# Macaron block on one core: normalized rows written by column blocks, and three small reorderings

## The chip, the cores and the metric

The kernel runs on one core of one Trainium2 chip. The metric is the device time of one execution in microseconds, as the median of several executions. A core has five engines that work side by side and wait for each other through semaphores: TensorE (PE, with its weight loads shown as PEld), VectorE (DVE), ScalarE (ACT), GpSimd (POOL) and SyncE (SP), which issues most of the DMAs. Each engine takes its instructions in the order in which they are written.

## What is computed

x is 2 sequences of 2048 tokens with 256 features, all in float32. LN is a layernorm without weights.

```
x1 = x  + 0.5 * ffn(LN(x))
x2 = x1 + attention(LN(x1))
x3 = x2 + 0.5 * ffn(LN(x2))

ffn(h):   prev = h shifted by one token (zero at a sequence's start)
          xr, xk = mu_r*h + (1-mu_r)*prev,  mu_k*h + (1-mu_k)*prev
          sigmoid(xr @ W_r.T) * (relu(xk @ W_k.T)**2 @ W_v.T)
attention(h), 16 heads of 16:
          q, k = relu(h @ Wq.T)/4, relu(h @ Wk.T)/4 ; v = h @ Wv.T ; u = silu(h @ Wu.T)
          kv = k.T @ v over the whole sequence (per head) ; o = q @ kv
          (o / rms(o) * u) @ Wo.T
```

## The kernel before

**Tiling.** The 4096 tokens are 8 blocks of 512 (4 token tiles of 128). A block passes through FFN 1, attention's projections and the sum over tokens; when a sequence's four blocks are summed, attention's output can follow, then FFN 2. An FFN instance has a number n: 0 to 7 is FFN 1 of block n, 8 to 15 is FFN 2 of block n - 8.

**Precision.** A product of two float32 operands is made of three products in the faster fp32r format. Each operand is split into a high part (a copy to fp32r, on ACT) and a low part (the difference, on POOL or DVE). The helper product (L1328, L1329, L1330) issues hi*hi, hi*lo and lo*hi. Names with _hi and _lo are these parts.

**The order of work** is written out by hand on each engine. In the loop over block i (1 to 5 on POOL, 1 to 6 on DVE and ACT) the pieces that matter here are:

- PE: ffn_k(i+1), waiting for g_acc of block i-1; transpose_b (rows of x1 turned); ffn_r; k_and_u (attention's k and u); ffn_v; gram(i-1), the sum over tokens of x1 times k; q_of. After block 3's gram, kv(0) multiplies the sum by Wv.
- ACT: activate_k (relu, then Square to act_hi), x2_high, previous (the shifted rows), sigmoids, mix_high, sigmoid_u and kt_high, normalize(i+2), x1_high(i) (waits for gram(i-1)), at i = 2 the high part of W_o (L848), relu_q.
- POOL: act_low(i) (two squares at L467, then two subtractions at L476), scales_a(i+2), k_low(i+1), kt_low(i-1), scales_b(i) (var_epsB, rstdB), x1_low(i), at i = 2 the low part of W_o (L573).
- DVE: stats_a, turn(i+1), x2_low, mix_current, silu, gate and add of FFN 1, stats_b(i), r_low(i+1) (two subtractions to mix_r_lo), at i = 3 the centring of Wv, keep_g(i-1) (L1091 and L1094: gram's PSUM result into g_acc).

**Turned rows.** For n = 3 to 6 the normalized rows xn are not transposed on PE. SP stores them to a DRAM buffer `spread` (L390) in two halves, and loads them back into `squares` (L397), so that DVE can turn blocks of 32x32 into PSUM (turn, L989). ACT wrote xn (L646), and turn's output is what previous and mix_current read.

Of the kernel before, what the change touches and what calls it, by code (L numbers as in the profile page):

```python
# [5 lines left out]
F32 = mybir.dt.float32  # L6
# [39 lines left out]
def macaron(nc, x, w_t, mu_r, mu_k, out):  # L46
# [6 lines left out]
    with ExitStack() as ctx:  # L53
# [200 lines left out]
        def tile_row(tile, block, t):  # L254
            return row(tile, block, t * D, D)
# [27 lines left out]
        def parts(n):  # L283


            return 2 * (n - 1)
# [14 lines left out]
        quads = squares[:].rearrange("p g e -> p (g e)")  # L301
        spread = nc.dram_tensor("spread", [len(TURNED), 2, QUADS, P, P], F32).ap()

        def half(g):
            return slice(g * D, (g + 1) * D)

# [52 lines left out]
        @block.sync  # L359
        def _(sp):  # L360
            def load_x(b):
                sp.dma_start(row(xs, b).rearrange("p (t d) -> p t d", t=TILES),
                             x[b * BLOCK:(b + 1) * BLOCK, :].rearrange("(t p) d -> p t d", p=P)
                             ).then_inc(s_x_in[b], 16)

            def store_x(b):
                sp.wait_ge(s_x3, 2 * (b + 1))
                sp.dma_start(out[b * BLOCK:(b + 1) * BLOCK, :].rearrange("(t p) d -> p t d", p=P),
                             row(xs, b).rearrange("p (t d) -> p t d", t=TILES)).then_inc(s_out, 16)


            for t in (0, 2):
                sp.dma_start(tile_row(xs, 0, t), x[t * P:(t + 1) * P, :]).then_inc(s_x0[t], 16)
            sp.dma_start(raw_ffn[:, 0, :, :], weight_rows("ffn_k")).then_inc(s_w_in["ffn_k"], 16)
            load_x(1)
            sp.dma_start(raw_ffn[:, 1, :, :], weight_rows("ffn_r")).then_inc(s_w_in["ffn_r"], 16)
            sp.dma_start(raw_att[:, 0, :, :], weight_rows("k")).then_inc(s_w_in["k"], 16)
            sp.dma_start(raw_att[:, 1, :, :], weight_rows("u")).then_inc(s_w_in["u"], 16)
            sp.dma_start(raw_ffn_v[:], weight_rows("ffn_v")).then_inc(s_w_in["ffn_v"], 16)
            sp.dma_start(raw_att[:, 2, :, :], weight_rows("q")).then_inc(s_w_in["q"], 16)  # L380
            sp.dma_start(wv[:], weight_rows("v")).then_inc(s_w_in["v"], 16)
            load_x(2)
            sp.dma_start(wo[:], weight_rows("o")).then_inc(s_w_in["o"], 16)
            for b in range(3, NB):
                load_x(b)
            for k, n in enumerate(TURNED):
                for g in range(2):

                    sp.wait_ge(*normalized(n, 2 * g + 1))
                    sp.dma_start(spread[k, g].rearrange("j p (q f) -> p q j f", f=QUAD),  # L390
                                 xn[:, 2 * g:2 * g + 2, :].rearrange("p t (h j f) -> p (t h) j f", h=HALVES, j=QUADS)
                                 ).then_inc(s_spread[g], 16)
                if k > 0:
                    sp.wait_ge(s_tA, 2 * n)
                for g in range(2):
                    sp.wait_ge(s_spread[g], 16 * (k + 1))
                    sp.dma_start(quads[:, g * BANK:(g + 1) * BANK],  # L397
                                 spread[k, g].rearrange("j (c i) e -> (j c) (i e)", i=QUADS)).then_inc(s_quads[g], 16)
            for b in range(NB - 1):
                store_x(b)  # L400
            for t in range(TILES):
                sp.wait_ge((s_x3_even, s_x3_odd)[t % 2], t // 2 + 1)
                sp.dma_start(out[(NB - 1) * BLOCK + t * P:(NB - 1) * BLOCK + (t + 1) * P, :],
                             tile_row(xs, NB - 1, t)).then_inc(s_out, 16)
            sp.wait_ge(s_out, 16 * (NB - 1 + TILES))
# [3 lines left out]
        def _(pool):  # L409
# [53 lines left out]

            def act_squares(n):
                for h in range(HALVES):
                    pool.wait_ge(s_act_hi, parts(n) + h + 1)
                    nc.gpsimd.tensor_tensor(act_k[:, h, :], act_k[:, h, :], act_k[:, h, :],  # L467
                                            ALU.mult).then_inc(s_sq, 1)

            def act_low(n, squares=True):  # L470
                if squares:
                    act_squares(n)
                for h in range(HALVES):

                    pool.wait_ge(s_sq, parts(n) + h + 1)
                    nc.gpsimd.tensor_tensor(act_lo[:, h, :], act_k[:, h, :], act_hi[:, h, :].bitcast(F32),  # L476
                                            ALU.subtract).then_inc(s_act_lo, 1)

# [22 lines left out]
            def kt_low(a):  # L501

                for g in range(2):
                    pool.wait_ge(s_kt_hi, 2 * (a - 1) + g + 1)
                    tiles = slice(2 * g, 2 * g + 2)
                    nc.gpsimd.tensor_tensor(k_lo[:, tiles, :], k_tok[:, tiles, :], k_hi[:, tiles, :].bitcast(F32),  # L506
                                            ALU.subtract).then_inc(s_kt_lo, 1)
# [53 lines left out]
            for i in range(1, 6):  # L561
                act_low(i)
                scales_a(i + 2)
                k_low(i + 1)
                if i > 1:
                    kt_low(i - 1)
                scales_b(i)
                x1_low(i)
                if i == 1:
                    weight_sum("v")  # L570
                if i == 2:
                    pool.wait_ge(s_wo_hi, 1)
                    nc.gpsimd.tensor_tensor(wo_lo[:], wo[:], wo_hi[:].bitcast(F32), ALU.subtract).then_inc(s_wo_lo, 1)  # L573
            norm_second(0)
            act_low(6)
            k_low(7)
# [45 lines left out]
        def _(act):  # L622
# [15 lines left out]
            def normalize(n, tiles=range(TILES)):  # L638
                b = FFN[n][1]
                act.wait_ge(s_lnA, 3 * n)  # L640
                if n > 0:
                    act.wait_ge(s_tA, 2 * n)
                for t in tiles:
                    if t in xn_vector.get(n, ()):
                        continue
                    nc.scalar.activation(xn[:, t, :], tile_row(xs, b, t), ACT.Identity,  # L646
                                         bias=shiftA[:, t:t + 1], scale=rstdA[:, t:t + 1]).then_inc(s_xn, 1)

            def first_column(n):
# [48 lines left out]
            def activate_k(n, halves=range(HALVES)):  # L698
                for h in halves:
                    act.wait_ge(s_k, 2 * n + h + 1)  # L700
                    if n == 1 and h == 0:

                        act.wait_ge(s_v, 2)
                    elif n > 0 and h == 0:
                        act.wait_ge(s_act_lo, lows(n - 1))
                    nc.scalar.activation(act_k[:, h, :], psK[:, h, :], ACT.Relu).then_inc(s_relu, 1)
                    act.wait_ge(s_relu, 2 * n + h + 1)
                    if n == 0:
                        nc.scalar.activation(act_k[:, h, :], act_k[:, h, :], ACT.Square).then_inc(s_act_first, 1)
                        continue  # L710
                    if n > 1 and h == 0:
                        act.wait_ge(s_v, 2 * n)
                    nc.scalar.activation(act_hi[:, h, :], act_k[:, h, :], ACT.Square).then_inc(s_act_hi, 1)

            def activate_k2(n):
                for h in range(HALVES):
# [110 lines left out]
            for i in range(1, 7):  # L827
                front(i, i + 1, i - 1)
                sigmoid_u(i - 1, 0)
                sigmoid_r(i, 1)  # L830
                sigmoid_u(i - 1, 1)
                if i > 1:
                    kt_high(i - 1, 0)
                sigmoid_u(i - 1, 2)
                sigmoid_u(i - 1, 3)
                if i > 1:
                    kt_high(i - 1, 1)
                if i == 6:
                    keep_g_rows(0)
                mix_high(i + 1, 1)  # L840
                if i <= 5:
                    normalize(i + 2)
                if i >= 5:
                    square_heads(i - 5)
                x1_high(i)
                if i == 2:
                    act.wait_ge(s_w_in["o"], 16)
                    nc.scalar.activation(wo_hi[:], wo[:], ACT.Identity).then_inc(s_wo_hi, 1)  # L848
                relu_q(i - 1)

            front(7, None, 6)
# [68 lines left out]
        def _(dve):  # L920
# [305 lines left out]
            for i in range(1, 7):  # L1226
# [15 lines left out]
                if i == 6:  # L1242
                    add_attention(0)
                stats_b(i)
                r_low(i + 1)
                if i == 3:
                    center_weight("v", 4)
                keep_g(i - 1)
                if i == 4:
                    mask_kv(0)  # L1250
                if i == 6:
# [474 lines left out]
```

## Time and profile before

| | |
|---|---|
| median of 3 runs | 307.89 us (307.72 to 310.2) |
| the profiled execution | 307.94 us, its span 306.2 us |
| TensorE clock granted | full speed in all 40 slices |
| DMA | 28416 packets, 15.05 MB, 17122 packets under 512 B |
| HBM written | 6.29 MB |

The span is the stretch that the profile covers; the execution's own time is 1.7 us more. In the views a PE instruction's duration is modelled and overlaps with the next one, so the distance from one start to the next is what shows PE's pace. Idle time in square brackets stands ahead of the instruction, with what released it.

### The profile page before, as it was taken

Reading aid. Unit: us, or ns where it says so; the run is one execution under the profiler, and the core shown is the slowest. Engines: PE = TensorE matmul, PEld = TensorE weight load, DVE = VectorE, ACT = ScalarE, POOL = GpSimd, SP = SyncE. Lnnn points to the kernel's source line nnn. Section 1 sums busy time; section 2 is a strip of 40 time slices with the busy share of each in tenths; the row PEclk is TensorE's granted clock in tenths of the full one; section 3 lists DMA queues with packets and bytes.
Section 4 is the critical chain, followed back from the end, with each engine's and each line's share of the span. In section 5 each row is a group of like instructions: output and inputs, shape, how many; then the busy total and the mean of one; then the engine's idle time right before and its main releaser. Section 6 shows DMA issues by size and latency. Waiting matters only on the chain.

```text
span 306.2 us, 5777 instructions
## 1 busy us (share of the span) xinstructions
PE 298.5 (97%) x2003; PEld 271.7 (89%) x2003; DVE 247.4 (81%) x601; ACT 235.5 (77%) x461; POOL 214.5 (70%) x237
## 2 busy tenths in 40 slices
PE   6999999999999999999999999999999999999995
PEld 4888879978988898998988998999999999999894
DVE  4899896677876966985993798596989798999695
ACT  3988949969779779689178368489797979699981
POOL 4598969779689489479168116736797979759823
PEclk9999999999999999999999999999999999999999
DMA  7950070070330510000000000000001101001123
GB/s 234 382 208 2 2 137 2 2 137 0 58 83 0 80 59 0 2 1 2 0 2 1 2 0 0 2 2 2 0 16 56 37 34 54 17 2 68 42 99 137
DMA packets 28416, 15.05 MB, mean 49 GB/s; under 512 B 17122, under 2 KB 27364, under 8 KB 28388
## 3 DMA queue, kind: packets, MB, share of 16 engines
q1 hardware_dynamic: 28096, 14.42, 16.7%
q8 instruction: 16, 0.26, 0.3%
q10 hardware_dynamic: 292, 0.26, 0.2%
q14 instruction: 12, 0.10, 0.1%
HBM read 8.39 MB, written 6.29 MB: 48 GB/s over the span
## 4 chain that ended last, share of the span: by engine, by line
PE 63%; DVE 16%; POOL 8%; ACT 7%; issue 3%; DMA 1%; ACTq 0%; DVEq 0%; POOLq 0%
PE psK L1328 6%; PE psX L1328 6%; PE psK L1330 6%; PE psK L1329 6%; PE psX L1330 6%; PE psX L1329 6%; PE psRV L1328 5%; PE psRV L1330 5%; PE psRV L1329 5%; DVE mix L978 3%; PE psA L1533 2%; PE psX L1546 2%; PE psK L1533 2%; PE psA L1345 2%; DVE gate L1054 2%
## 5 line engine op out<-in xcount | busy, mean ns | idle before, releaser
L978 DVE SCALAR_TENSOR_TENSOR mix<-psA,mu,mix 128x512 f32<-128x512 f32 x60 | 41.5, 744 | 10.0 <-ACT mix L663 10.0
L454 POOL TENSOR_TENSOR mix_k_lo<-mix,mix_k_hi 128x512 fp32r<-128x512 f32 x26 | 33.6, 1313 | 5.1 <-ACT mix_k_hi L696 5.1
L663 ACT ACTIVATE mix<-psA,one_mu 128x511 f32<-128x511 f32 x60 | 36.9, 697 | 0.0
L1328 PE MATMUL psRV<-ffn_hi,mix_r_hi 128*128 128x256 f32 x120 | 34.3, 286 | 0.0
L1330 PE MATMUL psRV<-ffn_hi,mix_r_lo 128*128 128x256 f32 x120 | 33.6, 280 | 0.0
L1329 PE MATMUL psRV<-ffn_lo,mix_r_hi 128*128 128x256 f32 x120 | 33.5, 279 | 0.0
L646 ACT ACTIVATE xn<-xs,shiftA,rstdA 128x256 f32<-128x256 f32 x53 | 27.9, 623 | 2.6 <-POOL shiftA L438 2.6
L1328 PE MATMUL psRV<-ffn_hi,act_hi 128*128 128x256 f32 x96 | 27.6, 287 | 0.2 <-POOL act_lo L476 0.2
L1330 PE MATMUL psRV<-ffn_hi,act_lo 128*128 128x256 f32 x96 | 26.8, 279 | 0.0
L1329 PE MATMUL psRV<-ffn_lo,act_hi 128*128 128x256 f32 x96 | 26.8, 279 | 0.0
L947 DVE BATCH_NORM_STATS2 statsA<-xs 128x6 f32<-128x256 f32 x64 | 22.4, 412 | 2.7 <-DMA xs<-x_dram 2.6
L1328 PE MATMUL psK<-mix_k_hi,ffn_hi 128*128 128x512 f32 x60 | 24.2, 404 | 0.2
L442 POOL TENSOR_SCALAR var_epsB<-meanvarB 128x4 f32<-128x4 f32 x8 | 4.0, 498 | 28.5 <-DVE meanvarB L972 28.5
L497 POOL TENSOR_TENSOR x_lo<-xs,x_hi 128x512 fp32r<-128x512 f32 x14 | 17.8, 1295 | 8.3 <-ACT x_hi L746 8.3
L1330 PE MATMUL psK<-mix_k_hi,ffn_lo 128*128 128x512 f32 x60 | 23.5, 392 | 0.0
L1329 PE MATMUL psK<-mix_k_lo,ffn_hi 128*128 128x512 f32 x60 | 23.5, 391 | 0.0
L1328 PEld LDWEIGHTS psRV<-ffn_hi,mix_r_hi 128*128 128x128 f32 x120 | 22.5, 187 | 0.5 <-issue 0.2
L1329 PEld LDWEIGHTS psRV<-ffn_lo,mix_r_hi 128*128 128x128 f32 x120 | 22.6, 188 | 0.2
L1330 PEld LDWEIGHTS psRV<-ffn_hi,mix_r_lo 128*128 128x128 f32 x120 | 22.5, 188 | 0.0
L506 POOL TENSOR_TENSOR k_lo<-k_tok,k_hi 128x512 fp32r<-128x512 f32 x14 | 18.5, 1328 | 4.4 <-ACT k_hi L751 4.3
L696 ACT ACTIVATE mix_k_hi<-mix 128x512 fp32r<-128x512 f32 x30 | 18.9, 659 | 1.9 <-DVE mix L978 1.8
L1328 PEld LDWEIGHTS psRV<-ffn_hi,act_hi 128*128 128x128 f32 x96 | 18.0, 188 | 0.7 <-POOL act_lo L476 0.4
(211 smaller groups left out, 1086.5 us busy)
## 6 DMA issues: line engine op xcount, KB each, us to landing
xs<-x_dram SPq DMA_DIRECT2D x7, 512.0 KB, 7.8
out_dram<-xs SPq DMA_DIRECT2D x7, 512.0 KB, 2.8
spread<-xn SPq DMA_DIRECT2D x8, 256.0 KB, 4.5
squares<-spread SPq DMA_DIRECT2D x8, 256.0 KB, 2.7
out_dram<-xs SPq DMA_DIRECT2D x4, 128.0 KB, 1.7
xs<-x_dram ACTq DMA_DIRECT2D x2, 128.0 KB, 3.1
xs<-x_dram SPq DMA_DIRECT2D x2, 128.0 KB, 2.8
silu_u<-w_ffn_k_dram SPq DMA_DIRECT2D x1, 256.0 KB, 4.0
```

Of the source, the lines that this page charges most:

```text
L454: nc.gpsimd.tensor_tensor(mix_k_lo[:, h, :], mix[:, 0, h, :], mix_k_hi[:, h, :].bitcast(F32), ALU.subtract).then_inc(s_lo_k, 1)
L497: nc.gpsimd.tensor_tensor(x1_lo[:, g * BANK:(g + 1) * BANK], row(xs, a, g * BANK, BANK), x1_hi[:, g * BANK:(g + 1) * BANK].bitcast(F32), A ...
L506: nc.gpsimd.tensor_tensor(k_lo[:, tiles, :], k_tok[:, tiles, :], k_hi[:, tiles, :].bitcast(F32), ALU.subtract).then_inc(s_kt_lo, 1)
L646: nc.scalar.activation(xn[:, t, :], tile_row(xs, b, t), ACT.Identity, bias=shiftA[:, t:t + 1], scale=rstdA[:, t:t + 1]).then_inc(s_xn, 1)
L663: nc.scalar.activation(mix[:, rk, h, 1:BLOCK], psA[:, h, 0:BLOCK - 1], ACT.Copy, scale=one_mu[:, rk, h:h + 1]).then_inc(s_prev, 1)
L696: nc.scalar.activation(hi[:, h, :], mix[:, rk, h, :], ACT.Identity).then_inc(done, 1)
L947: nc.vector.bn_stats(statsA[:, t, :], tile_row(xs, b, t)).then_inc(s_bnA, 1)
L978: nc.vector.scalar_tensor_tensor(out=m, in0=psA[:, h, :], scalar=mu[:, rk, h:h + 1], in1=m, op0=ALU.mult, op1=ALU.add).then_inc(s_mix, 1)
L1328: nc.tensor.matmul(dst, a_hi, b_hi, start=start, stop=False)
L1329: nc.tensor.matmul(dst, a_hi, b_lo, start=False, stop=False)
L1330: return nc.tensor.matmul(dst, a_lo, b_hi, start=False, stop=stop)
L1533: last = nc.tensor.matmul(ps[:, t // 2, (t % 2) * D + h * P:(t % 2) * D + (h + 1) * P], q_half(j, h)[:, tok(t)], kv_bd[:, j // BB, h, :], ...
```

## The change

- xn of n = 3 to 6 is written by ACT in another order: instead of a token tile's 256 features in a row, feature h*128 + j*32 + f goes to block j, so that block j of two token tiles lies in 128 neighbouring elements. The store then moves one piece of 128 elements (512 bytes) per partition and j, where it moved four of 32 elements. What lands in `spread` is the same.
- keep_g(i-1) stands ahead of r_low(i+1) (and of the centring of Wv) on DVE.
- The high part of W_o stands ahead of x1_high(2) on ACT, the low part ahead of scales_b(2) on POOL.
- Of FFN 1's instance n = 1, the second half's square in act_k is done by ACT behind act_hi, not by POOL. POOL's later waits on its own squares count one less.

```diff
+        def spread_rows(t):
+            return xn[:].rearrange("p t d -> p (t d)").rearrange("p (g j t h f) -> p g t h j f", g=2, j=QUADS, t=2, h=HALVES
+                                                                 )[:, t // 2, t % 2, :, :, :]
...
-                    sp.dma_start(spread[k, g].rearrange("j p (q f) -> p q j f", f=QUAD),
-                                 xn[:, 2 * g:2 * g + 2, :].rearrange("p t (h j f) -> p (t h) j f", h=HALVES, j=QUADS)
+                    sp.dma_start(spread[k, g].rearrange("j p e -> p j e"),
+                                 xn[:, 2 * g:2 * g + 2, :].rearrange("p t d -> p (t d)").rearrange("p (j e) -> p j e", j=QUADS)
                                  ).then_inc(s_spread[g], 16)
...
             def act_squares(n):
                 for h in range(HALVES):
+                    if (n, h) == (1, 1):
+                        continue
                     pool.wait_ge(s_act_hi, parts(n) + h + 1)
...
-                    pool.wait_ge(s_sq, parts(n) + h + 1)
+                    if (n, h) == (1, 1):
+                        pool.wait_ge(s_act_first, HALVES + 1)
+                    else:
+                        pool.wait_ge(s_sq, parts(n) + h + 1 - (n > 1))
...
                 if i > 1:
                     kt_low(i - 1)
+                if i == 2:
+                    pool.wait_ge(s_wo_hi, 1)
+                    nc.gpsimd.tensor_tensor(wo_lo[:], wo[:], wo_hi[:].bitcast(F32), ALU.subtract).then_inc(s_wo_lo, 1)
                 scales_b(i)
                 x1_low(i)
                 if i == 1:
                     weight_sum("v")
-                if i == 2:
-                    pool.wait_ge(s_wo_hi, 1)
-                    nc.gpsimd.tensor_tensor(wo_lo[:], wo[:], wo_hi[:].bitcast(F32), ALU.subtract).then_inc(s_wo_lo, 1)
...
-                    nc.scalar.activation(xn[:, t, :], tile_row(xs, b, t), ACT.Identity,
+                    given, rows = tile_row(xs, b, t), xn[:, t, :]
+                    if n in TURNED:
+                        given, rows = given.rearrange("p (h j f) -> p h j f", h=HALVES, j=QUADS), spread_rows(t)
+                    nc.scalar.activation(rows, given, ACT.Identity,
                                          bias=shiftA[:, t:t + 1], scale=rstdA[:, t:t + 1]).then_inc(s_xn, 1)
...
                     nc.scalar.activation(act_hi[:, h, :], act_k[:, h, :], ACT.Square).then_inc(s_act_hi, 1)
+                    if (n, h) == (1, 1):
+                        act.wait_ge(s_act_hi, HALVES)
+                        nc.scalar.activation(act_k[:, h, :], act_k[:, h, :], ACT.Square).then_inc(s_act_first, 1)
...
-                x1_high(i)
                 if i == 2:
                     act.wait_ge(s_w_in["o"], 16)
                     nc.scalar.activation(wo_hi[:], wo[:], ACT.Identity).then_inc(s_wo_hi, 1)
+                x1_high(i)
                 relu_q(i - 1)
...
                 stats_b(i)
+                keep_g(i - 1)
                 r_low(i + 1)
                 if i == 3:
                     center_weight("v", 4)
-                keep_g(i - 1)
```

## Rows read from the trace of the kernel before

**Rows 1.** The page: busy time, share of the span and instructions

```profile
PE 298.5 (97%) x2003; PEld 271.7 (89%) x2003; DVE 247.4 (81%) x601; ACT 235.5 (77%) x461; POOL 214.5 (70%) x237
```

**Rows 2.** Timelines of POOL and PE, gram(1): start us, us, line, tiles, count

```profile
58.13 1.31 POOL L506 TENSOR_TENSOR k_lo<-k_tok,k_hi 128x512 fp32r<-128x512 f32 x1
...
59.59 0.28 PE L1330 MATMUL psK<-k_hi,x_lo 128*128 128x256 f32 x1
59.70 0.28 PE L1328 MATMUL psK<-k_hi,x_hi 128*128 128x256 f32 x1
```

**Rows 3.** Timeline of PE in ffn_v(1)

```profile
34.66 0.28 PE L1330 MATMUL psRV<-ffn_hi,act_lo 128*128 128x256 f32 x1
35.18 0.39 PE L1328 MATMUL psRV<-ffn_hi,act_hi 128*128 128x256 f32 x1 [0.24 <-POOL act_lo L476]
35.41 0.28 PE L1329 MATMUL psRV<-ffn_lo,act_hi 128*128 128x256 f32 x1
```

**Rows 4.** Timeline of PE from q_of(0) to ffn_k(2); PE and weight load at ffn_k(3)

```profile
43.51 0.39 PE L1329 MATMUL psX<-x_lo,att_hi 128*128 128x512 f32 x1
43.74 0.39 PE L1330 MATMUL psX<-x_hi,att_lo 128*128 128x512 f32 x1
44.17 0.50 PE L1328 MATMUL psK<-mix_k_hi,ffn_hi 128*128 128x512 f32 x1
...
64.35 0.39 PE L1330 MATMUL psX<-x_hi,att_lo 128*128 128x512 f32 x1
64.87 0.19 PEld L1328 LDWEIGHTS psK<-mix_k_hi,ffn_hi 128*128 128x128 f32 x1 [0.55 <-DVE g_acc L1094]
```

**Rows 5.** Timeline of PE in gram(2)

```profile
80.77 0.28 PE L1330 MATMUL psK<-k_hi,x_lo 128*128 128x256 f32 x1
81.20 0.39 PE L1328 MATMUL psK<-k_hi,x_hi 128*128 128x256 f32 x1 [0.15 <-POOL k_lo L506]
```

**Rows 6.** Timeline of PE from q_of(3) to kv(0)

```profile
106.23 0.39 PE L1330 MATMUL psX<-x_hi,att_lo 128*128 128x512 f32 x1
106.70 0.68 PE L1511 MATMUL psA<-wv,g_acc 128*128 128x128 f32 x4
```

**Rows 7.** Timeline of POOL, act_low(1)

```profile
30.56 2.04 POOL L467 TENSOR_TENSOR act_k<-act_k 128x512 f32<-128x512 f32 x2
```

**Rows 8.** Timeline of ACT in block 1; groups by line and shape

```profile
27.31 0.63 ACT L713 ACTIVATE act_hi<-act_k 128x512 fp32r<-128x512 f32 x1
...
L635 ACT ACTIVATE att_hi<-q_store 128x512 fp32r<-128x512 f32 x3 | 1.7, 613 | 0.0
```

**Rows 9.** Timeline of DVE in block 1

```profile
37.27 1.66 DVE L1061 TENSOR_TENSOR xs<-xs,gate 128x512 f32<-128x512 f32 x1
...
42.25 1.26 DVE L1019 TENSOR_TENSOR mix_r_lo<-mix,mix_r_hi 128x512 fp32r<-128x512 f32 x2
43.43 0.68 DVE L1091 COPY g_acc<-psK 128x512 f32<-128x512 f32 x1
```

**Rows 10.** Timelines of DVE and PE in block 6

```profile
151.41 1.26 DVE L1019 TENSOR_TENSOR mix_r_lo<-mix,mix_r_hi 128x512 fp32r<-128x512 f32 x2
...
151.83 0.38 PE L1533 MATMUL psA<-kv_bd,q_store 128*128 128x128 f32 x2
```

**Rows 11.** Timeline of POOL in block 2, then in block 7

```profile
63.13 0.54 POOL L442 TENSOR_SCALAR var_epsB<-meanvarB 128x4 f32<-128x4 f32 x1 [3.68 <-DVE meanvarB L972]
...
67.83 1.28 POOL L573 TENSOR_TENSOR wo_lo<-wo,wo_hi 128x512 fp32r<-128x512 f32 x1
...
177.34 0.20 POOL L442 TENSOR_SCALAR var_epsB<-meanvarB 128x4 f32<-128x4 f32 x1 [6.15 <-DVE meanvarB L972]
```

**Rows 12.** Timeline of ACT in block 2

```profile
62.08 1.06 ACT L746 ACTIVATE x_hi<-xs 128x1024 fp32r<-128x1024 f32 x1 [1.17 <-PE psK L1330]
```

**Rows 13.** DMA issues: KB each, median us from issue to landing

```profile
spread<-xn SPq DMA_DIRECT2D x8, 256.0 KB, 4.5
squares<-spread SPq DMA_DIRECT2D x8, 256.0 KB, 2.7
```

## Prediction

> **What bounds the kernel now.** I read the busy table first: TensorE 97% against 81, 77 and 70% for VectorE (DVE), ScalarE (ACT) and GpSimd (POOL) [rows 1]. Every product runs on TensorE (PE) and the change touches none, so only PE's gaps can be won. The modelled ends hide them: a 256-column product is listed with 0.28 us while the next starts 0.12 us later. So I went through PE's own timeline start to start. Undisturbed pitches are 0.12 us for 256 columns [rows 2] and, in the second gap's rows below, 0.23 us for 512. Starts of neighbours that I give without a group are read from the same engine's timeline and only place an instruction. From 30 to 120 us five gaps stand out:
>
> - 34.66 to 35.18: 0.52 us where 0.12 is usual, lost 0.40; the product behind it takes 0.23 instead of 0.12, 0.11 more. Releaser: act_lo on POOL [rows 3]. Together 0.51.
> - 43.74 to 44.17: 0.43 against 0.23, lost 0.20, plus the 0.11 of restart: 0.31. ffn_k(2) waits there for keep_g(0) [rows 4].
> - 64.35 to 64.87: 0.52 against 0.23, 0.29 + 0.11 = 0.40. ffn_k(3) waits for keep_g(1), the releaser of its weight load after 0.55 us idle [rows 4].
> - 80.77 to 81.20: 0.43 against 0.12, 0.31 + 0.11 = 0.42. gram(2) waits for the second k_lo on POOL [rows 5].
> - 106.23 to 106.70: 0.47 against 0.23, 0.24. kv(0) waits for keep_g(3) [rows 6]. I count no restart here, because kv's plain fp32 products have another pitch.
>
> Sum 0.51 + 0.31 + 0.40 + 0.42 + 0.24 = 1.88 us. Everything else that PE loses is in the opening (before 30 us) or after 220 us, where the change edits nothing. So 1.9 us, 0.6% of the time, is close to all that this change could win.
>
> **The change, part by part.**
>
> *One square of block 1 to ACT.* POOL now does two squares (2.04 us) and then two subtractions ahead of the first gap [rows 7]. Taking one square away (1.02 us) brings the second act_lo 1.0 us forward; PE wants it 0.51 earlier, so the gap closes whole: -0.51. On ACT the square costs one more Square of 128x512, 0.63 us [rows 8]; it follows act_hi at about 27.95 and ends near 28.6, three microseconds before POOL asks. Queued behind it are previous(2), the sigmoids and all of sigmoid_u(0). ACT has no idle time until its normalizations at 37.2, so they move by the 0.63. What consumes them: DVE's mix and silu, then gate_ffn(1). The gate starts at 36.55 having idled 0.57 for PE, so DVE absorbs most of the 0.63. gram(0) on PE needs k_tok, which ends at 35.1 now and 35.7 then, against a start at 37.8 less 0.5. Cost on the path: nothing; if that cover were gone, at most 0.63.
>
> *keep_g ahead of r_low.* In each block DVE runs two r_low subtractions (1.26 us) before keep_g (0.68 us) [rows 9]. The swap makes g_acc final 1.2 us earlier. The three waits that it feeds are short by 0.31, 0.40 and 0.24, so all three close: -0.95. What is put later is mix_r_lo, by 0.6 us, to about 44.1 in block 1, and its consumers (ffn_r(2) at 47.8, the copies of previous(3) at 49.4) are over three microseconds away. The added risk is that keep_g now waits for gram, with r_low, the statistics and the turn queued behind it on DVE. In blocks 1 to 5 gram is done before DVE gets there (block 1: gram ends about 41.1, DVE arrives at 42.25). In block 6 it is not: DVE arrives at 151.41 and PE leaves gram(5) at 151.83 [rows 10], so DVE idles about 0.55. The chain behind it ends in head_norms(1) and x2_low(6); k_and_u(6) wants x2_low only at 162.8, and it is done 0.4 before, after waiting 0.2 for ACT, so 0.6 of room against 0.55. I take 0, and up to +0.1 for the range.
>
> *W_o's split moved.* wo_lo (1.28 us) now stands in POOL's chain just ahead of act_squares(3), behind which k_low(4) and the late k_lo follow. In its new place, before scales_b(2), POOL has been idle for 3.68 us [rows 11]. wo_hi on ACT (a copy of 128x512, 0.61 us by the nearest row [rows 8]) goes in front of x1_high(2), where ACT idles 1.17 us for gram [rows 12], so x1_high starts when it did. wo_lo then runs from about 61.5 to 62.8, before var_epsB at 63.1. Both copies are hidden, with 0.3 us to spare on POOL. POOL becomes free 1.28 earlier, and the 0.42 gap closes: -0.42. If the 0.3 were missing, POOL would still gain over 0.9, so the gap closes anyway.
>
> *Rows by column blocks.* ACT writes the same 256 elements in runs of 32 instead of one run; the store's pieces go from 128 to 512 bytes, 2048 to 512 of them. For ACT's price the nearest row is a copy whose output is cut in runs (att_hi, two runs of 256): 0.61 us for 512 elements, where an uncut one takes 0.63 [rows 8]. I take no change; the bounds are 0 and, for runs 8 times shorter than that row shows, +0.1 us per write. Four writes then take 0.4 of the 1.2 us or more that ACT idles behind them, so still nothing on the path. For the store: it lands 4.5 us after issue, and the reload of the same bytes, in 2 KB pieces, 2.7 [rows 13]. I take about 3, between them and near the reload, so the turned rows arrive some 1.5 us earlier. DVE's waits for them go. None of it is PE time today, because x2_low behind the turn waits for ACT anyway. But PE reaches block 3 some 1.2 us earlier after the edits above, and without faster turned rows it would be short by about 0.3 there. So this edit is worth 0 alone and protects the others.
>
> The page "SBUF — State Buffer" of the Trainium skill (Reading the diagram) states that a VectorE instruction with two SBUF inputs and a GpSimd one that reads SBUF exclude each other for a whole instruction. The trace agrees: DVE's add at 37.27 takes 1.66 us instead of 0.69 while POOL runs k_low(2) [rows 9]. By that rule POOL's k_low(2), once it starts earlier, could block the add anew at another moment and the sum would be 306.7 (the second rival); by my reading of the row the overlap shrinks and the sum stays 306.0.
>
> **What is next late.** PE reaches gram(1) 0.82 us (0.51 + 0.31) earlier. Its third token tile starts at 59.7 now, 58.9 then, and the second k_lo runs from 58.13 for 1.31 us [rows 2], to 59.45. So k_lo must come 0.55 us earlier or a new gap opens. POOL's chain from block 1's second layernorm is solid work, so it must start that much earlier. Two things push that way. DVE's adds in block 1, which took 1.66 and about 1.0 us beside POOL, meet less of it, since k_low(2) starts and ends 1.0 earlier (my estimate is 0.5 us). And POOL's var_epsB takes 0.54 us when r_low runs on DVE beside it [rows 11], against 0.20 in block 7, where DVE runs an instruction that reads PSUM [rows 11]; keep_g reads PSUM too, so another 0.3 or so. Estimate 0.8, enough by a quarter of a microsecond.
>
> **Sum.** Against the profiled execution: 307.94 us (span 306.2, with 1.7 around it) - 0.51 - 0.95 - 0.42 = 306.06. The median of the runs shown is 307.89, 0.05 lower; so 306.0.
>
> **Rivals.**
> - *Faster than the sum.* An opening that moves, or a tail that closes: the late gaps (about 0.3 us near 223, three near 290 to 300 of together 0.8) belong to chains that shift with PE, so I see no cause. 305.3.
> - *The new wait at gram(1).* If POOL's chain in block 1 comes no earlier (DVE's adds blocked at other moments), 0.55 + 0.11 returns: 306.7. With the turned rows also no faster, 0.3 more: 307.0. For it: the margin is 0.25 and rests on contention. Against: var_epsB's shorter time alone gives half.
> - *Nothing.* The gaps are handed on, gate by gate, to the DVE-ACT chains that alternate from 275 us to the end in the chain view: 307.9. Against: PE starts stay at their pitch through almost all of 110 to 220 us, so PE itself sets when those chains begin.
> - *Slower.* ACT's writes in runs of 32 cost double: 0.5 us each, 2.1 us per block in blocks 1 to 4, against 1.2 us of idle time behind them, so x1_high, relu_q and through it the transposes of x1 come 0.9 late four times: +3.6, less 0.9 for the gaps that still close: 310.6. It decides from 0.3 us per write. The uncut and cut rows of ACT speak against it.
> - *The change doesn't do what it says:* pieces are 512 bytes but landing is latency, 4.5 stays; that is in the second rival.
>
> **Chances.** The forecast (306.0, give or take 0.4) 0.58; faster 0.07; the new wait 0.20; nothing 0.11; slower 0.04. A change within 1% (3.1 us) is about what a measurement of this kernel can't tell from none. Faster by over 1% would need 304.8, more than all the gaps: 0.03. Slower by over 1% needs 311.0, the slower rival at its upper end: 0.03. Same 0.94. The range leaves out the slower rival and part of "faster" and of "nothing": 305.3 to 307.8.
>
> **What the profile after would show.** Right: no PE gap before the second half of ffn_v(1), at ffn_k(2), ffn_k(3), the third tile of gram(2), or kv(0); wo_lo between kt_low(1) and var_epsB; var_epsB near 0.2 us in blocks 1 to 5; the store landing in 3 us with 512-byte packets; no DVE wait for squares; the xn writes still at 0.62. Wrong: a PE gap with k_lo as its releaser at gram(1) near 59, xn writes above 0.9 us, or a DVE idle of over 0.6 before keep_g(5) that reaches k_and_u(6).

## The result, and the profile after

The median of 16 runs is 306.73 us (305.67 to 308.03) against 308.98 us (307.48 to 310.39) for 16 runs of the kernel before on the same chip: ratio 0.9934, 95% interval 0.9912 to 0.9957. The profiled execution took 305.97 us with a span of 304.2, against 307.94 and 306.2. Forecast were 306.0 in a range of 305.3 to 307.8. The forecast started from 307.89, the median of three runs; over 16 runs the medians differ by 2.25 us and the lowest runs by 1.81, where 1.9 was forecast. The median of the kernel after falls between two clusters of runs (eight at 306.35 or less, eight at 307.11 or more; last section), and so does that of the kernel before.

The page of the kernel after, busy time, clock, packets and the chain that ended last:

```profile
PE 297.3 (98%) x2003; PEld 272.1 (89%) x2003; DVE 245.9 (81%) x601; ACT 236.0 (78%) x462; POOL 210.8 (69%) x236
...
PEclk9999999999999999999999999999999999999999
...
DMA packets 16128, 15.05 MB, mean 49 GB/s; under 512 B 738, under 2 KB 15076, under 8 KB 16100
...
PE 85%; DVE 8%; ACT 3%; issue 1%; DMA 1%; POOL 1%; DVEq 0%; ACTq 0%
...
spread<-xn SPq DMA_DIRECT2D x8, 256.0 KB, 3.4
squares<-spread SPq DMA_DIRECT2D x8, 256.0 KB, 2.7
```

TensorE's share hardly moves (97% to 98%, [rows 1]), but the gaps are gone. PE's own timeline of the kernel after, at the five places:

```profile
34.72 0.28 PE L1346 MATMUL psRV<-ffn_hi,act_lo 128*128 128x256 f32 x1
34.84 0.28 PE L1344 MATMUL psRV<-ffn_hi,act_hi 128*128 128x256 f32 x1
...
43.30 0.39 PE L1346 MATMUL psX<-x_hi,att_lo 128*128 128x512 f32 x1
43.52 0.39 PE L1344 MATMUL psK<-mix_k_hi,ffn_hi 128*128 128x512 f32 x1
...
63.58 0.39 PE L1346 MATMUL psX<-x_hi,att_lo 128*128 128x512 f32 x1
63.80 0.39 PE L1344 MATMUL psK<-mix_k_hi,ffn_hi 128*128 128x512 f32 x1
...
79.52 0.28 PE L1346 MATMUL psK<-k_hi,x_lo 128*128 128x256 f32 x1
79.64 0.28 PE L1344 MATMUL psK<-k_hi,x_hi 128*128 128x256 f32 x1
...
104.57 0.39 PE L1346 MATMUL psX<-x_hi,att_lo 128*128 128x512 f32 x1
104.80 0.83 PE L1527 MATMUL psA<-wv,g_acc 128*128 128x128 f32 x6
```

The starts are 0.12 us apart for 256 columns and 0.23 for 512, where 0.52, 0.43, 0.52, 0.43 and 0.47 stood [rows 3 to 6].

**The measure used below.** Executions of one program differ by about 2 us before FFN 1's block 1 (last section), so spans of single profiles can't be compared. I take the stretch from the start of the first product of ffn_k(1) to the start of the last product of all. In the timeline of the kernel after these are:

```profile
21.02 0.58 PE L1344 MATMUL psK<-mix_k_hi,ffn_hi 128*128 128x512 f32 x1
...
300.32 0.28 PE L1346 MATMUL psK<-ffn_hi,act_lo 128*128 128x256 f32 x1
```

279.30 us. In the kernel before the same two start at 20.98 and 302.29: 281.31. The stretch lost 2.01 us. "At +49.8" means 49.8 us after the first of the two. Both kernels issue the same products in the same order, and the difference of their starts grows in steps, all at the five places: 0.50 behind the ffn_v(1) gap, 0.80 behind ffn_k(2), 1.23 behind ffn_k(3) (1.28 soon after), 1.71 behind gram(2), 2.02 behind kv(0), and then constant within 0.06 to the end.

### The profile page after: what moved, and what is told of

Its sections match the earlier page's. It is cut to its first block, busy times and chain, and to the rows that moved or that the text cites. A ratio compares the mean times of both kernels' runs of the same rounds, so it can differ in the third digit from the quotient of the medians.

```text
span 304.2 us, 5777 instructions
## 1 busy us (share of the span) xinstructions
PE 297.3 (98%) x2003; PEld 272.1 (89%) x2003; DVE 245.9 (81%) x601; ACT 236.0 (78%) x462; POOL 210.8 (69%) x236
## 4 chain that ended last, share of the span: by engine, by line
PE 85%; DVE 8%; ACT 3%; issue 1%; DMA 1%; POOL 1%; DVEq 0%; ACTq 0%
PE psK L1344 8%; PE psK L1346 8%; PE psK L1345 8%; PE psX L1344 8%; PE psX L1346 8%; PE psX L1345 8%; PE psRV L1344 8%; PE psRV L1346 7%; PE psRV L1345 7%; PE psA L1361 3%; PE psA L1549 2%; PE psX L1562 2%; PE psX L1476 2%; PE psK L1549 2%; DVE mix L994 2%
## 5 line engine op out<-in xcount | busy, mean ns | idle before, releaser
L447 POOL TENSOR_SCALAR var_epsB<-meanvarB 128x4 f32<-128x4 f32 x8 | 1.9, 238 | 26.4 <-DVE meanvarB L988 26.4
L789 ACT ACTIVATE q_store<-psX 128x512 f32<-128x512 f32 x16 | 9.6, 598 | 12.1 <-PE psX L1346 12.1
```

## The experiments

| kernel | median, us | lowest run | ratio of times | first and last product | stretch |
|---|---|---|---|---|---|
| before | 308.98 | 307.48 | | 20.98, 302.29 | 281.31 |
| after | 306.73 | 305.67 | 0.9934 | 21.02, 300.32 | 279.30 |
| after_again | 305.9 | 305.74 | 0.9895 [0.986, 0.993] | 21.08, 300.32 | 279.24 |
| no_rows | 307.53 | 305.41 | 0.9951 [0.9922, 0.998] | 22.86, 302.61 | 279.75 |
| no_keep_g | 308.0 | 306.82 | 0.9983 [0.9956, 1.001] | 20.79, 301.14 | 280.35 |
| no_wo | 307.36 | 305.8 | 0.9953 [0.9926, 0.9979] | 22.39, 301.68 | 279.29 |
| no_square | 306.3 | 305.91 | 0.9933 [0.9911, 0.9955] | 21.05, 300.96 | 279.91 |
| only_rows | 307.87 | 307.62 | 1.0002 [0.9974, 1.0029] | | |
| only_keep_g | 308.06 | 306.36 | 0.9988 [0.9967, 1.0009] | 20.80, 300.73 | 279.93 |
| only_wo | 307.77 | 307.63 | 0.9987 [0.9964, 1.0009] | 20.77, 302.13 | 281.36 |
| only_square | 307.09 | 306.79 | 0.9981 [0.996, 1.0003] | 22.65, 303.07 | 280.42 |
| rows_keep_g | 306.67 | 306.01 | 0.992 [0.9891, 0.9949] | 22.90, 302.53 | 279.63 |
| twice | 309.15 | 307.06 | 0.9977 [0.9947, 1.0007] | 20.82, 301.64 | 280.82 |
| norm_first | 311.4 | 310.16 | 1.0066 [1.0042, 1.0089] | 20.80, 304.64 | 283.84 |

Where a kernel gains or loses under 1 us the stretch decides, and the lowest run supports it: it lies 26.0 to 26.5 us above the stretch in all but no_rows (25.66). The medians carry the 2 us of the opening too. Each ratio compares a kernel with runs of the kernel before taken beside it, not with the table's first row: medians 308.04 (lowest 307.64) for no_rows, no_keep_g, no_wo and no_square, 308.05 (307.55) for the only_ kernels, 309.65 (307.75) for the other four.

A wait costs PE twice: the distance to the product behind it, beyond the usual one, and a restart of about 0.11 us at the next (0.07 to 0.08 at kv(0) and k_and_u(2)). Such pairs are added up below.

**after_again**: the kernel after, unchanged. It repeats to 0.06 us. By the expectation below, the 0.46 us of no_rows would then be its edit's; what speaks against that stands at no_rows.

> The kernel after, unchanged, profiled once more to see how far the stretch from the first product of ffn_k(1) to the last product repeats. If profiles of one kernel repeat within 0.1 us: 279.2 to 279.4, and the 0.46 of the kernel without the rows edit is that edit's. If they don't: up to 279.8, and its 0.46 is no finding.

**no_keep_g**: all edits but one, r_low back ahead of keep_g.

```diff
-                keep_g(i - 1)
                 r_low(i + 1)
                 if i == 3:
                     center_weight("v", 4)
+                keep_g(i - 1)
```

> The changed kernel with keep_g behind r_low as before. Theory by the prediction's sum: the three waits of 0.31, 0.40 and 0.24 us come back, span 305.15. Shared-cover theory: the square moved to ACT already lets DVE's adds of block 1 pass POOL earlier by 0.8 us, so the first of the three hardly comes back (0.1 or less) and a gap of 0.2 to 0.4 us at gram(1) may open because var_epsB takes 0.54 us again; span about 305.0, with the gaps in other places than before. Rival (handed on): the waits reappear later anyway, span 304.2 to 304.4.

1.05 us longer than after, near the 0.95 of the prediction's sum, but by other gaps. Three waits for g_acc stand, with their restarts: 0.37 us at ffn_k(3), 0.30 at kv(0), and 0.41 at a place where the kernel before has none, ffn_k(4). PE's weight load there, in no_keep_g:

```profile
85.02 0.19 PEld L1344 LDWEIGHTS psK<-mix_k_hi,ffn_hi 128*128 128x128 f32 x1 [0.56 <-DVE g_acc L1110]
```

Of ffn_k(2)'s gap 0.05 is left (the first two products start at 43.22 and 43.50, where 0.23 is usual). The square covers the rest. gram(2) has no gap here either: W_o's move covers that one when the swap is missing.

**only_keep_g**: that edit alone.

```diff
+                keep_g(i - 1)
                 r_low(i + 1)
                 if i == 3:
                     center_weight("v", 4)
-                keep_g(i - 1)
```

> The kernel before with keep_g ahead of r_low alone. By the prediction's sum 0.95 us less, 280.35 from the first ffn_k(1) product to the last, with gram(2)'s gap of 0.42 still there. Shared-cover theory: var_epsB and rstdB on POOL get 0.5 us shorter in every block, so gram(2)'s gap shrinks too, to 0.3 or less: 280.1 to 280.25. Rival (handed on): 280.9 or more.

1.38 us of 2.01, more than any of the three accounts. All three g_acc waits are gone, and gram(2)'s gap too, which I had put down to W_o: POOL's second k_lo ends at +58.72 against +60.17 before, 1.45 us earlier, and PE comes only 0.88 earlier. A new gap stands at k_and_u(2). PE and DVE in only_keep_g:

```profile
70.30 0.28 PE L1330 MATMUL psRV<-ffn_hi,mix_r_lo 128*128 128x256 f32 x1
70.64 0.47 PE L1328 MATMUL psX<-att_hi,x_hi 128*128 128x512 f32 x1
```

```profile
67.11 0.79 DVE L989 STREAM_TRANSPOSE psA<-squares 128x256 f32<-128x256 f32 x2 [1.37 <-DMA squares<-spread]
68.54 0.79 DVE L989 STREAM_TRANSPOSE psA<-squares 128x256 f32<-128x256 f32 x2 [0.64 <-DMA squares<-spread]
69.24 1.26 DVE L1067 TENSOR_TENSOR x_lo<-psX,x_hi 128x512 fp32r<-128x512 f32 x2
```

0.34 us where 0.12 is usual. x2_low (x_lo in the rows, two of 1.26 us together) ends at 70.50, behind 2.01 us of waiting for the stored rows to come back.

**rows_keep_g**: before with the rows edit and this one (the spread_rows hunks of the diff, and only_keep_g's).

> Before, with the rows edit and the keep_g edit alone. With keep_g alone a new gap of 0.22 us stood at k_and_u(2), where VectorE waited 2.0 us for the spread rows to come back: 279.93 in all. If the rows edit protects it, that gap is gone and the opening gap of ffn_v(1) (0.36 and 0.10) stays: 279.65 to 279.75. If it protects nothing: 279.9 to 280.0. If my forecast's 0.3 us at block 3 was right: 279.6.

279.63: 0.30 less than only_keep_g, all of it at k_and_u(2). DVE in rows_keep_g:

```profile
68.90 1.44 DVE L997 STREAM_TRANSPOSE psA<-squares 128x256 f32<-128x256 f32 x4 [1.11 <-DMA squares<-spread]
70.75 1.29 DVE L1075 TENSOR_TENSOR x_lo<-psX,x_hi 128x512 fp32r<-128x512 f32 x2 [0.41 <-ACT x_hi L749]
```

One wait of 1.11 us instead of two of together 2.01, and x2_low waits for ACT.

**no_rows**: the other three edits, without the rows.

```diff
-                    sp.dma_start(spread[k, g].rearrange("j p e -> p j e"),
+                    sp.dma_start(spread[k, g].rearrange("j p (q f) -> p q j f", f=QUAD),
...
-                    if n in TURNED:
-                        given, rows = given.rearrange("p (h j f) -> p h j f", h=HALVES, j=QUADS), spread_rows(t)
```

> The changed kernel with xn written and stored as before (128-byte pieces); the other three parts kept. Theory (this part is worth nothing alone but protects the others): PE now reaches block 3 about 1.3 us earlier while the turned rows come as late as before, so x2_low(2) on DVE ends near 70.4 us and k_and_u(2), due at 70.2, opens a PE gap of 0.3 to 0.5 us; the gain falls from 2.0 to about 1.55 us (span 304.6 to 304.7). Rival (the turned rows never set PE's pace): no gap, span 304.2, while DVE again waits over 3 us for squares. A second rival (the rows are the main gain): span 305.5 or more.

The waits for the rows are back; x2_low in no_rows ends at 71.96, and PE starts k_and_u(2) at 72.12, on time. DVE in no_rows:

```profile
68.56 0.79 DVE L997 STREAM_TRANSPOSE psA<-squares 128x256 f32<-128x256 f32 x2 [1.24 <-DMA squares<-spread]
70.01 0.79 DVE L997 STREAM_TRANSPOSE psA<-squares 128x256 f32<-128x256 f32 x2 [0.66 <-DMA squares<-spread]
70.70 1.26 DVE L1075 TENSOR_TENSOR x_lo<-psX,x_hi 128x512 fp32r<-128x512 f32 x2
```

Counted from ffn_k(1) the first of these starts at +45.70, in only_keep_g at +46.31. The rows' chain begins at ACT's writes, and ACT follows PE: the writes start at +37.00 here and at +37.40 in only_keep_g, which is 0.40 of the 0.61; store and reload together took 0.2 less. That is why the edit protects nothing here. The cover is thin, though: x2_low ends 0.16 us before k_and_u(2) starts. The stretch is 0.45 longer all the same, but in no gap: 0.06 at one product of k_and_u(2), the rest crept in by nanoseconds per product, as in two kernels that have the rows edit (last section). It has the size that the theory gave, and not its cause. The lowest timed run, 305.41, is below that of after. So no cost of leaving the edit out is shown, and up to 0.45 us isn't excluded.

**only_rows**: the rows edit alone (no_rows' diff read backwards). Its profiled execution took 424.62 us at a mean granted clock of 0.66, so it has no stretch, and only its other times are used.

> The kernel before with xn's column blocks and 512-byte pieces alone. From the first ffn_k(1) product to the last product PE takes 281.3 us in the kernel before. Theory: PE's five gaps stay as they are, 281.3 give or take 0.1; the waits of DVE for squares (3.3 us) fall under 0.5. Rival (turned rows matter by themselves): 280.9 or less.

307.87 against 308.05 in the median and 307.62 against 307.55 in the lowest run, each beside the kernel before: no gain that these times could show. The interval leaves 0.9 us either way. What the expectation says of PE's gaps and of DVE's waits isn't shown.

**no_square** and **only_square**: POOL's square of block 1 kept, or that edit alone.

```diff
-                    if (n, h) == (1, 1):
-                        act.wait_ge(s_act_hi, HALVES)
-                        nc.scalar.activation(act_k[:, h, :], act_k[:, h, :], ACT.Square).then_inc(s_act_first, 1)
```

> The changed kernel with both squares of block 1 on POOL again. Theory: PE's first gap of 0.51 us at ffn_v(1) is back as before and nothing else, span 304.7. Shared-cover rival: since POOL is 1 us later in block 1, DVE's adds wait for it as before, and a part of the wait for keep_g(0) would show as well, in all 0.6 us or more, span 304.8 or more. Rival (ACT's extra 0.63 us had a price of its own in block 1): less than 0.5 is lost, span 304.5 or under.

> The kernel before with the one square on ACT alone. By the prediction's sum 0.51 us less, 280.8 from the first ffn_k(1) product to the last. Shared-cover theory: POOL leaves block 1 a microsecond earlier, DVE's adds there get through 0.8 us earlier, and so keep_g(0) is in time for ffn_k(2) without the swap: 0.51 + 0.31, 280.5. Rival (ACT's added 0.63 us is paid on PE): 281.0 or more.

PE in no_square, the first gap as before:

```profile
34.74 0.28 PE L1338 MATMUL psRV<-ffn_hi,act_lo 128*128 128x256 f32 x1
35.23 0.39 PE L1336 MATMUL psRV<-ffn_hi,act_hi 128*128 128x256 f32 x1 [0.21 <-POOL act_lo L481]
```

0.37 lost at the wait and 0.11 behind it, and no other gap; the other 0.13 of no_square's 0.61 is creep (last section), not the shared wait of the rival. Alone the square shortens the stretch by 0.89: 0.52 at its own gap, 0.22 at ffn_k(2), where 0.09 is left, and 0.15 in drifts without a gap. DVE in only_square, where the kernel before has 1.66 us [rows 9]:

```profile
38.83 0.93 DVE L1069 TENSOR_TENSOR xs<-xs,gate 128x512 f32<-128x512 f32 x1
```

This add runs beside POOL's k_low(2). It takes 0.92 to 0.94 us in after, no_keep_g and only_square, where POOL has one square less ahead of it, and 1.67 in no_square. So g_acc is final at +22.30 instead of +23.14. ffn_k(2)'s wait goes whole with the swap and for the most part with the square.

**no_wo** and **only_wo**: W_o's split left where it was, or moved alone.

```diff
-                x1_high(i)
                 if i == 2:
                     act.wait_ge(s_w_in["o"], 16)
                     nc.scalar.activation(wo_hi[:], wo[:], ACT.Identity).then_inc(s_wo_hi, 1)
+                x1_high(i)
...
-                if i == 2:
-                    pool.wait_ge(s_wo_hi, 1)
-                    nc.gpsimd.tensor_tensor(wo_lo[:], wo[:], wo_hi[:].bitcast(F32), ALU.subtract).then_inc(s_wo_lo, 1)
                 scales_b(i)
```

> The changed kernel with W_o's split in its old places on ACT and POOL. Theory by the prediction's sum: gram(2)'s gap of 0.42 us comes back, span 304.6. Shared-cover theory: keep_g ahead of r_low shortens var_epsB and rstdB on POOL by 0.66 us in every block, so the second k_lo of block 2 ends near 79.5 us, just before PE wants it at 79.6; the gap is 0.1 us or none, span 304.2 to 304.3. Rival: more than 0.42 us, because PE is 1.2 us earlier at gram(2) while POOL keeps its old time; span 305 or more.

> The kernel before with W_o's split moved alone. Both theories: gram(2)'s gap of 0.42 us closes and nothing else, 280.9 from the first ffn_k(1) product to the last. Rival (wo_lo in POOL's idle time pushes var_epsB, or wo_hi pushes x1_high): 281.1 or more, with var_epsB of block 2 later than 63.1 us.

no_wo equals after: 279.29 against 279.30. POOL in no_wo still does wo_lo in its old place:

```profile
67.79 1.27 POOL L583 TENSOR_TENSOR wo_lo<-wo,wo_hi 128x512 fp32r<-128x512 f32 x1
...
78.09 2.55 POOL L516 TENSOR_TENSOR k_lo<-k_tok,k_hi 128x512 fp32r<-128x512 f32 x2
```

wo_lo starts at +45.40; before, it started at +46.85 [rows 11], 1.45 us later. The two k_lo take 2.55 us where the timeline of before has 3.01, so the second ends 1.91 us earlier (80.64, +58.25; before 81.14, +60.16). PE comes 1.28 us earlier. The 0.63 between them covers the 0.31 that PE stood waiting at gram(2). In after, where wo_lo has moved, the second k_lo ends at +57.78, another 0.47 earlier, and PE has no use for it. only_wo closes the gap at gram(2) and hands it on. PE in only_wo, at ffn_k(4):

```profile
85.32 0.39 PE L1330 MATMUL psX<-x_hi,att_lo 128*128 128x512 f32 x1
85.84 0.51 PE L1328 MATMUL psK<-mix_k_hi,ffn_hi 128*128 128x512 f32 x1
86.18 0.40 PE L1329 MATMUL psK<-mix_k_lo,ffn_hi 128*128 128x512 f32 x1
```

0.52 for 0.23, and 0.34 for 0.23: 0.40 lost, at the place where no_keep_g waits for g_acc. In sum the move gains nothing, alone or on top of the rest. No account of only_wo had that: var_epsB of block 2 isn't late (62.94 us), so the rival has the time right and not the cause.

**twice**: after, with ACT's 16 turned writes doubled, so that ACT is charged the time that the slower rival charged. No instruction reads the extra results.

```diff
+                    if n in TURNED:
+                        c = (n - TURNED[0]) * TILES + t
+                        if c == 0:
+                            act.wait_ge(s_ffn_lo[2], 1)
+                        if c > 1:
+                            act.wait_ge(s_twice, c - 1)
+                        nc.scalar.activation(raw_ffn_v[:, t % 2, :].rearrange("p (h j f) -> p h j f", h=HALVES, j=QUADS), given,
+                                             ACT.Identity, bias=shiftA[:, t:t + 1], scale=rstdA[:, t:t + 1]).then_inc(s_twice, 1)
                     nc.scalar.activation(rows, given, ACT.Identity,
```

> The kernel after, with every turned normalization write (16 of them, blocks 3 to 6 of the work order) issued twice on ScalarE, the extra one of the same shape and of the same runs of 32, to memory nobody reads. It charges ScalarE about 0.5 us per write, 2 us per block. My slower rival's account (each 0.5 us beyond 0.3 of room reaches PE through x1's first rows): gaps of together 2.7 to 3.6 us, 282.0 to 282.9 between the first product of ffn_k(1) and the last product, against 279.3. Cover account (ScalarE's idle time in front of its waits for PE takes most of it): under 1 us, 279.3 to 280.3. The spread lies between the second and the rest: the listed write stays near 0.63 us in both.

The stretch is 1.52 us longer, between the two accounts, and by neither's mechanism: 1.4 of it is lost at gram(2), and the three other blocks have no gap. POOL, then ACT, in twice:

```profile
62.35 1.76 POOL L580 TENSOR_TENSOR wo_lo<-wo,wo_hi 128x512 fp32r<-128x512 f32 x1 [4.16 <-ACT wo_hi L872]
64.20 0.52 POOL L448 TENSOR_SCALAR var_epsB<-meanvarB 128x4 f32<-128x4 f32 x1
...
77.61 2.98 POOL L517 TENSOR_TENSOR k_lo<-k_tok,k_hi 128x512 fp32r<-128x512 f32 x2
```

```profile
61.13 0.62 ACT L668 ACTIVATE xn<-xs,shiftA,rstdA 128x256 f32<-128x256 f32 x1
61.63 0.65 ACT L872 ACTIVATE wo_hi<-wo 128x512 fp32r<-128x512 f32 x1
```

The same in after, POOL:

```profile
60.73 1.30 POOL L579 TENSOR_TENSOR wo_lo<-wo,wo_hi 128x512 fp32r<-128x512 f32 x1 [2.21 <-ACT wo_hi L863]
62.20 0.20 POOL L447 TENSOR_SCALAR var_epsB<-meanvarB 128x4 f32<-128x4 f32 x1 [0.17 <-DVE meanvarB L988]
```

ACT's two microseconds push wo_hi back, wo_lo meets r_low on DVE (both slow down: wo_lo takes 1.76 for 1.30, and the two r_low 2.39, where they take 1.28 at this place in after), and var_epsB behind it starts 2.2 us later, counted from ffn_k(1). k_lo ends at 80.59, and PE loses 0.83 us before gram(2)'s third tile (starts at 79.69 and 80.64), after 0.42 at the first. In this run the moved split is the one place where ACT's time is short; the margin of 0.3 us that I gave it was real (0.30 of idle time in only_wo), and small (0.17 in after).

**norm_first**, a try at what is left: in the last three attention blocks the head norms ahead of the statistics.

```diff
-                if n > 8:
-                    scales_a(n + 2)
                 norm_second(n - 5)
+                if n > 8:
+                    scales_a(n + 2)
...
-                    stats_a(n + 2)
                 head_norms(j, n > 8)
+                if n > 8:
+                    stats_a(n + 2)
```

> The kernel after, with the head norms ahead of the statistics in the three late attention blocks on VectorE, and GpSimd's half of the norm ahead of the scales there. What is left of PE's gaps before the tail is 0.29 and 0.11 us where TensorE transposes gout and waits for GpSimd's half. Gaps-are-chains account: both close and nothing else moves, 278.9 to 279.0 instead of 279.3. Handed-on account: the statistics come 2.8 us later, VectorE and ScalarE reach the next mix late, and as much or more opens there: 279.3 to 281.

The two gaps close (by +200.7 it is 0.29 us ahead of after, and 0.13 comes back at +233.2), and from +202.5 it loses 1.6 to 1.7 us in each of three blocks, 4.5 us at the end. PE in norm_first:

```profile
223.96 0.36 PE L1345 MATMUL psRV<-ffn_hi,act_hi 128*128 128x256 f32 x1 [0.51 <-POOL act_lo L533]
...
225.12 0.39 PE L1345 MATMUL psRV<-ffn_hi,act_hi 128*128 128x256 f32 x1 [0.56 <-POOL act_lo L533]
```

POOL now waits for the statistics (0.76 us at 220.62) with act_lo queued behind the scales. The gaps are handed on, at ten times the price, and over twice what the handed-on account allowed.

## Why the prediction was right, and where its reasons were not

- *The five gaps close and nothing opens:* right. 2.01 us against a sum of 1.88. Each step measured 0.50, 0.30, 0.43, 0.43 and 0.31 beside 0.51, 0.31, 0.40, 0.42 and 0.24; the last one's excess is the restart that I had left out at kv(0) (0.08: kv's first products started 0.19 apart before, 0.11 after). The sum was right; which edit each term belongs to was not.
- *The square, -0.51:* right in size as the last edit to be added (0.48 of no_square's 0.61; the rest has the small creep of the last section). Alone it shortens the stretch by 0.89, since most of ffn_k(2)'s wait also goes, through DVE's add in block 1. I had that faster add in the working, but only for gram(1). The forecast named one gap per edit; this 0.31 belongs to either of two.
- *The swap, -0.95:* this term was mis-sized. It is worth 1.38 alone and 1.05 on top of the rest. Alone it takes gram(2)'s gap along. On top of the rest it no longer has ffn_k(2)'s, but without it a wait at ffn_k(4) appears that the kernel before hides behind its other gaps. One reason shows in POOL's rows, in which the statistics no longer meet r_low on DVE. POOL and DVE of after, block 1:

```profile
41.63 0.20 POOL L447 TENSOR_SCALAR var_epsB<-meanvarB 128x4 f32<-128x4 f32 x1 [2.35 <-DVE meanvarB L988]
41.91 1.01 POOL L450 TENSOR_TENSOR rstdB<-var_epsB,minus_half 128x4 f32<-128x4 f32 x1
43.00 0.38 POOL L452 TENSOR_TENSOR rstd2B<-rstdB 128x4 f32<-128x4 f32 x1
```

```profile
41.46 0.66 DVE L1107 COPY g_acc<-psK 128x512 f32<-128x512 f32 x1
42.03 1.29 DVE L1035 TENSOR_TENSOR mix_r_lo<-mix,mix_r_hi 128x512 fp32r<-128x512 f32 x2
```

  var_epsB takes 0.20 where it took 0.54 and rstdB 1.01 where it took 1.33; rstd2B gives 0.18 back. That is 0.48 us of POOL's chain in a block, foretold at "another 0.3 or so" for one gap only. Of the 1.91 us by which no_wo's POOL comes earlier at gram(2), 0.49 is this, 0.46 the shorter k_lo, and 0.96 stands already at var_epsB(2) (63.58 in no_wo, 63.13 before [rows 11]).
- *W_o, -0.42:* the step failed that made this term an addend of its own. The swap alone closes the gap that I gave it. The move alone closes it too, but the wait at ffn_k(4), 0.40 us, takes its place: nothing is won in either case. Its account of POOL, free 1.28 us earlier, was nearly right: in only_wo POOL starts act_squares(3) 1.13 earlier, its second square then waits 0.34 for ACT, and the first k_lo of gram(2) starts 0.75 earlier.
- *Rows, 0 alone but 0.3 of protection at block 3:* 0 alone holds, as far as timed runs can show. The 0.30 is real at k_and_u(2), but was seen only where the swap stands without the square and W_o; which of these two matters wasn't separated. With them PE's earlier pace pulls ACT's normalization and the store forward. The step that failed held the turned rows fixed in time while PE moved; they are in PE's own chain. DVE's waits for the stored rows went as foretold, from 3.3 us to none, and the landing came to 3.4 us from 4.5, where I took 3. ACT's writes in runs of 32 cost nothing: the last three of the first turned block take 586 ns each in rows_keep_g, which has these runs, and 585 in only_keep_g, which has none. (In after they take 640, but so they do in no_rows without the runs.) This leaves the slower rival without its premise.

The page "SBUF — State Buffer" of the Trainium skill (Reading the diagram) says that a VectorE instruction with two SBUF inputs and a GpSimd one that reads SBUF shut each other out. The traces agree: wo_lo beside r_low in twice (1.76 us for 1.30, 2.39 for 1.28), and DVE's add in block 1 (1.66 us, or 0.93 where it meets less of k_low(2)).

- *The new wait at gram(1):* did not come. POOL's second k_lo there ends at 58.52 (55.87 + 2.65) and PE takes the third tile at 58.93. The gain, estimated as 0.8 us, was 0.96 counted from ffn_k(1), with DVE's add at 0.92 instead of 1.66 [rows 9]. The measured median, 306.73, is by chance this rival's 306.7: it lies outside the 306.0 give or take 0.4, because it falls between the clusters of short and long openings, where no run lies.
- *Block 6:* DVE waits 0.54 us before keep_g(5), as worked out (0.55), and no PE gap follows.
- *Nothing* and *faster*: neither came. The kernel after is 2.02 us ahead behind kv(0) and stays so within 0.06 to the end, so the gaps weren't handed on and the late gaps stayed as they were. In the chain that ended last PE has 85%, where it had 63% before.

## What to carry to other kernels

Gaps on the bounding engine aren't additive terms with one edit each: closing an early one moves every chain that follows that engine, and an edit that frees a second engine can close gaps that it wasn't made for, and bring others to light. Only leave-one-out and one-alone runs told which edit was worth its place; here W_o's move is worth nothing and adds a spot where ScalarE's time is short, and the rows gained 0.30 us beside the swap alone and nothing shown beside all three. Before crediting a faster transfer, ask whether its start moves with the consumer; before reordering to close a 0.3 us gap, list what stands behind the moved instruction on every queue, as norm_first's loss of 4.5 us shows.

## What the runs showed of the hardware

**The opening has two lengths.** The runs of one program form two clusters 1.8 to 2.0 us apart (before near 307.8 and 309.8, after near 305.8 and 307.6), and the profiles place most of it in ffn_k(0). After, then no_rows, 16 products of the same shape:

```profile
8.14 3.69 PE L1386 MATMUL psK<-mix,silu_u 128*128 128x256 f32 x16 [0.19 <-DVE mix L1014]
```

```profile
8.61 5.05 PE L1378 MATMUL psK<-mix,silu_u 128*128 128x256 f32 x16
```

The distance of starts is 216 ns at TensorE's full clock (2.4 GHz) and 427 ns, twice that, where the clock is at its lower level (1.2 GHz). In after all 15 distances but the first (291 ns) are near 216; in no_rows the first six are 427 and the seventh 380. That is 1.4 of the 1.8 us by which no_rows comes later to ffn_k(1) (22.86 against 21.02); the other 0.47 stands ahead of these products. The full level is granted later there. The views don't show it (1.00 from 8 to 12 us in both), because they count time ahead of the trace's first clock record as full speed. The records kept in the traces do: the full level begins at 11.49 us in no_rows, 10.89 in no_wo, 11.18 in only_square and 11.97 in rows_keep_g, and the first of the 16 products at the full pitch starts at 11.55, 11.09, 11.35 and 12.03. These four have the long opening. In the nine other profiles used here the record begins between 5.5 and 7.6 us, ahead of the first of these products, and the opening is the short one. Since runs of one program show both lengths, it is the execution's, not the edit's, and what decides it is open.

**A pitch that creeps.** Between +86 and +120 the mean distance of successive 512-column products is 227.2 or 227.3 ns in after, after_again, no_wo, only_keep_g, rows_keep_g and norm_first, 227.4 in before, 227.8 in no_keep_g, only_wo and only_square, and 228.6 to 228.8 in no_rows, no_square and twice. In the last three most of the excess lies in the products of k_and_u (psX<-att_hi,x_hi above all, many at 236 ns where after has 227). Two of the last three kernels have the rows edit, so it isn't that edit's. It makes up nearly all of no_rows' 0.45 us, so differences of the stretch under 0.5 us count here only where a gap shows them. No wait is shown for the creep, and it stays open whether it is the program's or the execution's; no_rows' lowest run speaks for the execution.
